# Odd chunks' tile products of the upper merge levels in the other column group

## The reference, cut to what matters

```python
def step(S, inps):
    qt, kt, vt, at, bt = inps
    Sk = jnp.einsum('bhvk,bhk->bhv', S, kt)
    err = Sk - vt
    S = at[..., None, None] * S - bt[..., None, None] * (err[..., None] * kt[:, :, None, :])
    ot = jnp.einsum('bhvk,bhk->bhv', S, qt)
    return (S, ot)
```

## Time and profile before

| | us |
|---|---|
| median of 3 runs | 3938.99 (3938.63 to 3939.24) |
| profiled execution, its own time | 3939.13 |
| its span | 3937.5 |
| granted TensorE clock over the span | 0.988 of full speed |
| PE busy | 3830.4 (97%) |
| PEld busy | 3139.7 (80%) |
| DVE busy | 2688.1 (68%) |
| ACT busy | 2117.1 (54%) |
| POOL busy | 1282.2 (33%) |

### The profile page before, as it was taken

The page is one execution under the profiler, slowest core; times in us unless marked ns, Lnnn a source line. Parts: engine busy times, 40 slices in busy tenths (PEclk is TensorE's granted clock), DMA queues, the critical chain, the costliest instruction groups (busy, mean ns, idle before and its releaser), DMA issues. The chain is left out here.

```text
span 3937.5 us, 119111 instructions
## 1 busy us (share of the span) xinstructions
PE 3830.4 (97%) x41088; PEld 3139.7 (80%) x41088; DVE 2688.1 (68%) x6942; ACT 2117.1 (54%) x5248; POOL 1282.2 (33%) x2594
## 2 busy tenths in 40 slices
PE   7999889999999999999999999999999999987999
PEld 5777668888888888888888888888888888876887
DVE  3444367777777777777777777777777777763222
ACT  3433346666666666666656666666666666642111
POOL 3434423333333333333333333333333333320000
PEclk9999989999999999999999999999999999997999
DMA  3344331111111211111221111111111121105543
GB/s 133 110 152 142 117 119 46 49 45 47 45 45 47 55 48 48 45 47 48 86 89 48 45 45 49 46 46 46 45 47 48 45 47 45 45 28 158 146 146 110
DMA packets 371785, 275.67 MB, mean 70 GB/s; under 512 B 153456, under 2 KB 284528, under 8 KB 369360
## 3 DMA queue, kind: packets, MB, share of 16 engines
q1 hardware_dynamic: 368848, 261.29, 23.1%
q0 software_dynamic: 2560, 8.39, 0.6%
HBM read 209.85 MB, written 59.77 MB: 68 GB/s over the span
## 5 line engine op out<-in xcount | busy, mean ns | idle before, releaser
L1284 PE MATMUL bank<-hx_hi,w_hi 128*128 128x512 f32 x2048 | 875.4, 427 | 27.6 <-POOL w_lo L909 23.9
L1284 PE MATMUL bank<-hx_hi,w_lo 128*128 128x512 f32 x2048 | 902.1, 440 | 0.0
L1284 PE MATMUL bank<-hx_lo,w_hi 128*128 128x512 f32 x2048 | 881.9, 431 | 0.0
L1080 DVE SCALAR_TENSOR_TENSOR conv<-bank,tap,conv 128x512 f32<-128x512 f32 x1152 | 854.8, 742 | 29.0 <-ACT conv L1222 10.9
L927 POOL TENSOR_TENSOR prods<-Lb,Tc 128x28 f32<-128x28 f32 (+6 forms) x896 | 203.8, 227 | 753.5 <-ACT Lb L1208 691.0
L1284 PEld LDWEIGHTS bank<-hx_hi,w_hi 128*128 128x128 f32 x2048 | 391.6, 191 | 62.9 <-issue 39.4
L1284 PEld LDWEIGHTS bank<-hx_lo,w_hi 128*128 128x128 f32 x2048 | 389.2, 190 | 51.5
L1284 PEld LDWEIGHTS bank<-hx_hi,w_lo 128*128 128x128 f32 x2048 | 390.0, 190 | 40.4
L961 POOL TENSOR_TENSOR oG<-oT,gT 128x512 f32<-128x512 f32 x128 | 163.9, 1281 | 664.9 <-ACT oT L1243 664.9
L1033 DVE SCALAR_TENSOR_TENSOR S<-S,gamma,bank 128x128 f32<-128x128 f32 x480 | 163.6, 341 | 232.0 <-PE bank L1363 223.8
L1196 ACT ACTIVATE Wc<-bank 128x128 f32<-128x128 f32 x512 | 141.7, 277 | 274.1 <-PE bank L1354 263.3
(11 more groups left out here) (156 smaller groups left out, 8718.3 us busy)
## 6 DMA issues: line engine op xcount, KB each, us to landing
gamma<-gamma_d SPq DMA_DIRECT2D x128, 258.0 KB, 3.3
alpha<-alpha_d SPq DMA_DIRECT2D x128, 256.0 KB, 3.3
oT_d<-oG SPq DMA_DIRECT2D x128, 256.0 KB, 2.4
o_raw<-oT_d SPq DMA_DIRECT2D x32, 1024.0 KB, 6.8
gu_raw<-in_gate_up SPq DMA_DIRECT2D x17, 1408.0 KB, 6.2
dn_raw<-in_down SPq DMA_DIRECT2D x17, 512.0 KB, 4.5
x_in<-in_x SPq DMA_DIRECT2D x8, 1024.0 KB, 9.2
w_raw<-in_Wk SPq DMA_DIRECT2D x32, 256.0 KB, 3.9
```

The lines of the kernel that those rows point to most:

```text
L1080: dve.scalar_tensor_tensor(out=conv[i][:, to], in0=PJ[PJ_OF[(g + 3) % 4][i]][:], scalar=tap[:, i, j + 1:j + 2], in1=conv[i][:, to], op0=AL ...
L1284: last = pe.matmul(dst, a[:, i, k], b[:, k, cols], start=(j == 0), stop=(j == 3 * KC - 1))
```

## The change

In visits 0 to 3 the products of odd chunks (c = 1, 3) write the other column group: in visit 0 quadrants 0 and 2 in place of 1 and 3, in visit 1 quadrants 1 and 3 in place of 0 and 2, in visit 2 partitions 0 to 63, in visit 3 partitions 64 to 127. The operands, and so the rows of the array, stay as they were. An odd chunk shares the columns of WH with the even one before it (`half(c)`), so that WH is half as wide. Each copy on ACT becomes two, one for the even chunks, which stays on its partitions, and one for the odd ones, which reads the other partitions of WH and writes those of MT or TT that it wrote before. The semaphores count twice as far. No instruction changes its place in a queue.

```diff
+        def half(c):
+
+            return c // 2
...
-                        dve.wait_ge(tt64_done, at(2, 1, 1))
+                        dve.wait_ge(tt64_done, at(4, 1, 2))
...
-                wh = WH[:, 0:GT // 2].rearrange("p (c t) -> p c t", c=G)
+                wh = WH[:, 0:GT // 4].rearrange("p (c t) -> p c t", c=G // 2)
...
                         if k == 0:
                             for u in (1, 3):
-                                act.activation(MT[quad(u), :, 0:TB], wh[quad(u), :, 0:TB], ACT.Copy).then_inc(mt32_done, 1)
+                                for odd in range(2):
+                                    act.activation(MT[quad(u), odd::2, 0:TB], wh[quad(u - odd), :, 0:TB], ACT.Copy)\
+                                       .then_inc(mt32_done, 1)
                         if k == 1:
                             for u in (0, 2):
-                                act.activation(TT[quad(u), par, :, quad(u + 1)], wh[quad(u), :, 0:TB], ACT.Copy, scale=-1.0)\
-                                   .then_inc(tt64_done, 1)
+                                for odd in range(2):
+                                    act.activation(TT[quad(u), par, odd::2, quad(u + 1)], wh[quad(u + odd), :, 0:TB], ACT.Copy,
+                                                   scale=-1.0).then_inc(tt64_done, 1)
                         if k == 2:
-                            act.activation(MT[64:128], wh[64:128], ACT.Copy).then_inc(mt64_done, 1)
+                            for odd in range(2):
+                                rows = slice(0, 64) if odd else slice(64, 128)
+                                act.activation(MT[64:128, odd::2], wh[rows], ACT.Copy).then_inc(mt64_done, 1)
                         if k == 3:
-                            act.activation(TT[0:64, par, :, 64:128], wh[0:64], ACT.Copy, scale=-1.0)\
-                               .then_inc(tt128_done, 1)
+                            for odd in range(2):
+                                rows = slice(64, 128) if odd else slice(0, 64)
+                                act.activation(TT[0:64, par, odd::2, 64:128], wh[rows], ACT.Copy, scale=-1.0)\
+                                   .then_inc(tt128_done, 1)
...
                             if v in (0, 1):
-                                cols = slice(c * 64, c * 64 + TB)
+                                cols = slice(half(c) * 64, half(c) * 64 + TB)
                                 for u in (0, 2):
                                     lo, hi = quad(u), quad(u + 1)
                                     if v == 0:
-                                        last = pe.matmul(WH[hi, cols], LT[lo, (g + 1) % 4, c, hi], Tnb[lo, par, c],
+                                        last = pe.matmul(WH[lo if c % 2 else hi, cols], LT[lo, (g + 1) % 4, c, hi],
+                                                         Tnb[lo, par, c], start=True, stop=True)
+                                    else:
+                                        last = pe.matmul(WH[hi if c % 2 else lo, cols], MT[hi, c, 0:TB], TTb[hi, par, c],
                                                          start=True, stop=True)
-                                    else:
-                                        last = pe.matmul(WH[lo, cols], MT[hi, c, 0:TB], TTb[hi, par, c],
-                                                         start=True, stop=True)
+                            cols = slice(half(c) * 64, half(c) * 64 + 64)
+                            low, high = slice(0, 64), slice(64, 128)
                             if v == 2:
-                                last = pe.matmul(WH[64:128, c * 64:c * 64 + 64], LT[0:64, (g + 1) % 4, c, 64:128], Tn64[:, c],
+                                last = pe.matmul(WH[low if c % 2 else high, cols], LT[low, (g + 1) % 4, c, high], Tn64[:, c],
                                                  start=True, stop=True)
                             if v == 3:
-                                last = pe.matmul(WH[0:64, c * 64:c * 64 + 64], MT[64:128, c], TT[64:128, par, c, 64:128],
+                                last = pe.matmul(WH[high if c % 2 else low, cols], MT[high, c], TT[high, par, c, high],
                                                  start=True, stop=True)
```

More of the change, by code:

```diff
@@ L1297, in visit_waits @@
                         pe.wait_ge(tn_done, at(3, 2))
-                        wait(pe, tt128_done, at(1, 1))
+                        wait(pe, tt128_done, at(2, 1))
                     if late and v == 1:
-                        pe.wait_ge(mt32_done, at(2, 2))
+                        pe.wait_ge(mt32_done, at(4, 2))
                     if late and v == 2:
-                        pe.wait_ge(tt64_done, at(2, 2))
+                        pe.wait_ge(tt64_done, at(4, 2))
                         pe.wait_ge(tn64_done, at(1, 2))
@@ L1305, in visit_waits @@
                     if late and v == 3:
-                        pe.wait_ge(mt64_done, at(1, 2))
+                        pe.wait_ge(mt64_done, at(2, 2))
                         pe.wait_ge(placed, at(4, 2))
@@ L1352, in chain_step @@
                         if c == 0:
-                            pe.wait_ge(tt128_done, at(1, 1))
+                            pe.wait_ge(tt128_done, at(2, 1))
                         pe.matmul(w[:, D:2 * D], TT[:, cur, c], R[:], start=True, stop=True).then_inc(chain_done, 1)
```

## The result

The changed kernel took 3924.07 us (median of 6 runs, 3920.63 to 3926.69); the kernel before took 3938.81 in the same session (3935.62 to 3943.20). The ratio is 0.9964, with a 95% interval of 0.9953 to 0.9975: faster by 14.7 us, where 32 had been forecast. The profiled execution took 3925.09, with a span of 3923.5.

A forecast was written before the change was run, and what follows sets the result against it. TensorE was taken as the bound, busy 23.40 us of a 23.40 turn. Three turns of -0.36 and one of +0.07 make -1.01 a head, -32 over 32 heads, from 3939.13 to 3907; own range 3895 to 3925, 8-in-10 range 3878 to 3950.

The forecast's parts named there:

- rival 1: TensorE's column groups of one row group take turns, so PE gains nothing while ACT is late: 3953 us, slower; chance 0.14.
- The saving of visits 0 and 1: Sixteen late 32x32 passes on four tiles instead of two, at the diagonal's 8 ns: 0.14 us less in each visit.
- the sum: Three turns of -0.36 us and one of +0.07 make -1.01 a head, times 32 heads -32 us: 3907.
- ScalarE's copies: Six copies a turn become twelve, about 212 and 268 ns each: +0.37 us at the first copy place, +0.36 at the second.
- rival 3: ACT's copies overlap or cost nothing extra, so visits 0, 1 and 3 count, 0.51 us a turn: 3874; chance 0.15.
- Rival 2: Halved copies on ACT cost as much as whole ones, 0.29 us each, or the shift costs something: 3952, slower; chance 0.12.
- Step 1: After visit 0, 0.14 us shorter, ACT ends its copies 0.23 later; DVE's convolution waits for L1222 and is 0.18 late.
- Steps 2 to 4: Ordinary turn from S at 2032.29 to L1421: visit 1's gain pays for the late convolution; PE stays 0.14 us early.
- Step 5: Visit 2, between L1363 and L1421: its 0.23 us turns into waiting for Lx at L1421 and is lost.
- Step 6: Visit 3, after L1421: DVE waits for PE behind it, so its 0.23 us stays; the turn is 0.37 shorter, 0.36 used.
- The turn of group 3 reads like this one: The turn of group 3 was taken to behave as the ordinary turn, 0.36 us shorter.
- The turn of group 0: ACT has no gap up to Wc; L1361 loads 0.30 us later, only visit 3's 0.23 comes off: 0.07 longer.

The follow-up runs named there:

- the doubling: Visit 0's sixteen late passes done twice, in the kernel before and in the changed one; single runs took 3968.68 and 3929.75 us.
- The experiment with the upper visits alone: Against the kernel before, only visits 2 and 3 use both column groups; visits 0 and 1 and their copies as before: 3914.66 us, ratio 0.9940.
- The experiment with the longer code: The changed kernel with visit 3's eight late passes done twice in the turn of group 1, so 16 instructions more: 3920.82 us, a single run.
- the run with the lower visits alone: Against the kernel before, only visits 0 and 1 use both column groups, with eight halved copies; visits 2 and 3 as before: 3951.36 us, ratio 1.0035.

## Why the prediction was right or wrong, point by point

- **Do two column groups of one row group run together? Right**, and rival 1 is out: visit 2 halves, 0.46 to 0.23. By the rule of the Trainium skill that spoke for rival 1 (TensorE: Matmul & The Clock Gate, Part 3, that weight loads overlap with matmuls in flight only when the row group differs) nothing would have been won; it differs from the measurement, which decides. The row that was chosen to decide this, the first late pass among the diagonal's last, had told it truly, though it shows an overlap of a single pass.
- **The saving of visits 0 and 1 was mis-sized:** 0.14 each in the sum, 0.09 measured. The pace of 8 ns was right, as the doubling shows; a row of sixteen passes has a start and an end that cost 0.06. That such a start stands in the passes before too, and doesn't get shorter with more tiles, was left out.
- **ScalarE's copies: right in size** (215 and 210 for 212 ns, 270 and 272 for 268) **and in serial order**, with a reason that the prediction had not: straight halves overlap (four take 0.67) and cost the kernel nothing, as rival 3 says, and shifted ones don't (0.93, where 0.95 was forecast). Rival 2 is out by its mean of 268 ns.
- **Step 1, right:** DVE's convolution starts late behind the copies; its waits for this tap (L1222, now L1233) went from 10.9 us in 4 waits to 56.4 in 129.
- **Steps 2 to 4, right in sum.** The second chain product L1348, the one of the earlier trace rows, and what follows are 0.1 to 0.18 early against the turn's start where 0.14 was said; of two visits' gains about one is paid to the late convolution.
- **Step 5, right:** the wait at L1434 is 0.70 a turn for "about 0.7"; visit 2's gain is lost.
- **Step 6, right in three turns of four.** The experiment with the upper visits alone has -0.29, -0.26 and -0.24 where 0.23 was said.
- **"The turn of group 3 reads like this one" was the step that failed.** The sum gave it -0.36, and it was -0.03, which is 0.33 of the 0.48 us a head. The turn holds the loop's back branch, which the prediction did not price. In both kernels the branch starts 1.97 us behind the base matmul's last pass and 0.13 us behind visit 3's first weight load, so TensorE works off most of visit 3 while the branch runs. The row that would have warned was the 0.59 us idle by "issue" ahead of L1284 at 2067.98, in the kernel before. The branch was not covered then (1.92 us against 1.72), so what visit 3 saved came out as pause: from the base matmul to the turn's end 0.23 was forecast as saved and 0.07 was lost. The experiment with the longer code shows it: with the same work in it the turn is 0.39 shorter in the mean, and in the iterations with a short branch it is as long as that of group 2.
- **The turn of group 0: right in kind, wrong in place and size.** Forecast was +0.30 at L1361 for Wc, less visit 3's 0.23. In the changed kernel ScalarE is late already at oT (L1254), which frees the bank of L1429. ScalarE in order of time, that turn:

```profile
2071.71 0.77 ACT L1254 ACTIVATE oT<-bank,lnb,lnw 128x512 f32<-128x512 f32 x1
```

and TensorE's weight loads:

```profile
2071.64 0.42 PEld L1367 LDWEIGHTS bank<-R,TT 128*128 128x128 f32 x2
2072.60 0.97 PEld L1429 LDWEIGHTS bank<-kT 128*128 128x128 f32 x8 [0.54 <-issue]
```

oT ends at 2072.48 and the load follows at 2072.60. Before, oT ended 0.33 ahead of that load, 0.2 more than a hand-over needs, and no wait showed it; the prediction had followed ScalarE's queue only as far as Wc. Counted from the turn's start oT is 0.64 late (0.54 was forecast for ScalarE there), and the load 0.43. 0.43 less 0.23 is the median's +0.20.
- **The sum's sign, order and range held;** the size is less than half, by one turn that was taken to be like the others.

What stays open: where the 9 us at the ends of the run with the lower visits alone come from, at which lengths of code the branch is short, and why iterations of one kernel differ in it.

## What to carry to other kernels

Where a loop's turns look alike, read the one with the back branch by itself: a pause by "issue" at its edge says that what is queued on TensorE does not cover the branch, and then work saved in that queue is worth nothing, while work saved before the branch starts still counts (here 0.10 us). Splitting a copy is cheap on ScalarE as long as neighbours read and write the same partitions; a layout in which a copy reads other partitions than the one before it costs each copy in full, and the engine's queue must be followed to every bank that it frees, also those that nobody waits for yet. A pair of gains is best tried apart: here one half of the change was worth more than the whole.

## What the runs showed of the hardware that was not expected

- ScalarE starts a copy 0.12 us after the one before it if both have the same input and output partitions (32x64, 0.20 us long), and 0.24 after it if the input's partitions differ.
- TensorE's back branch over a body of 1316 to 1384 sequencer records and 1176 to 1240 passes took either 0.36 us or 1.1 to 2.5 (3.4 to 5.2 in one iteration of each kernel); at 1316 to 1320 records it was never the short one, with 16 instructions more in 12 to 22 of 29 iterations, with 128 more in 2 and in 7.
- Sixteen satisfied waits put among the matmuls added no record to the sequencer's and no time.
